# Packed value parts, and edge words turned by DMA instead of TensorE, in a two-layer graph kernel

## The reference, cut to what matters

```python
feats   = einsum('bnf,hfu->bhnu', X, W)                      # 8 heads x 64
dense   = leaky_relu(e_self[:, None] + e_neigh[None, :], 0.2)
att     = softmax(dense + NEG_BIG * (1 - A), axis=-1)        # over neighbours
x       = layernorm(x + relu(att @ feats + b))
deg     = sum(adj, axis=-1)
agg     = (adj @ x) / maximum(deg, 1e-6)
x       = layernorm(x + relu(concat([x, agg]) @ W1.T))
```

## Time and profile before

| | us |
|---|---|
| median of three runs | 3538.81 (3531.39 to 3540.57) |
| the profiled execution | 3539.05 |
| its span on the core | 3537.1 |
| PE busy | 3394.3 (96%) |
| DVE busy | 2461.7 (70%) |
| ACT busy | 1872.3 (53%) |
| POOL busy | 285.1 (8%) |
| mean granted TensorE clock | 0.986 |

### The profile page before, as it was taken

How to read it: one execution, slowest core, us unless ns; L and a number is a source line. 1 busy time by engine, 2 the same in 40 slices (tenths; PEclk the granted TensorE clock), 3 DMA queues, 4 the chain that set the end, 5 groups by cost and what they waited for, 6 DMA issues and landing times.

```text
span 3537.1 us, 135243 instructions
## 1 busy us (share of the span) xinstructions
PE 3394.3 (96%) x58432; PEld 2886.4 (82%) x58432; DVE 2461.7 (70%) x4364; ACT 1872.3 (53%) x2441; POOL 285.1 (8%) x252
## 2 busy tenths in 40 slices
PE   5999999999999999999999999999999999999998
PEld 4978879787796877968789697896978879788795
DVE  4857668576685766858678585785857758576685
ACT  3736546364464645636456363563736537365463
POOL 0020200202001020010201002010020200202001
PEclk9999999999999999999999999999999999999999
DMA  4113031130311303122031220312203131130310
GB/s 170 52 31 128 27 115 57 36 114 23 115 58 46 107 21 118 54 64 89 23 124 45 75 84 20 127 39 83 77 25 128 33 108 52 31 128 27 96 34 24
DMA packets 98396, 248.37 MB, mean 70 GB/s; under 512 B 14720, under 2 KB 14720, under 8 KB 97792
## 3 DMA queue, kind: packets, MB, share of 16 engines
q1 hardware_dynamic: 97792, 239.38, 20.6%
HBM read 205.26 MB, written 34.08 MB: 68 GB/s over the span
## 4 chain that ended last, share of the span: by engine, by line
PE 82%; DVE 9%; issue 5%; DMA 2%; ACT 2%; SPq 0%; DVEq 0%; ACTq 0%; POOL 0%; POOLq 0%
PE six L859 69%; PE pair L859 9%; DVE xs L738 2%; DVE stats L743 2%; PE six L996 2%; DVE feat L630 1%; DMA out_dram<-mask 1%; PE pair L888 1%; PE six L888 1%; DVE rs L751 0%; PE pair L897 0%; ACT x_parts L472 0%; DVE trl L619 0%; PE six L897 0%; DVE nb L753 0%
## 5 line engine op out<-in xcount | busy, mean ns | idle before, releaser
L859 PE MATMUL six<-rest,mask 128*128 128x65 bf16 x16384 | 1554.6, 194 | 3.1 <-issue 2.6
L859 PE MATMUL six<-x_parts,mask 128*128 128x65 bf16 x16384 | 1554.1, 193 | 2.2 <-issue 0.8
L859 PE MATMUL six<-third,mask 128*128 128x65 bf16 x16384 | 1554.1, 193 | 0.2
L859 PEld LDWEIGHTS six<-x_parts,mask 128*128 128x128 fp8e4 x16384 | 1538.2, 97 | 9.7 <-issue 8.0
L859 PEld LDWEIGHTS six<-rest,mask 128*128 128x128 fp8e4 x16384 | 1534.3, 97 | 6.8 <-issue 4.6
L859 PEld LDWEIGHTS six<-third,mask 128*128 128x128 fp8e4 x16384 | 1537.7, 97 | 0.0
L450 ACT ACTIVATE step<-s_bc,n_step 128x1024 uint16<-128x1024 f32 x1024 | 1092.1, 1138 | 369.7 <-DVE mask L688 369.0
L688 DVE TENSOR_TENSOR mask<-adj_t,step 128x1024 uint16<-128x1024 uint16 x1024 | 651.3, 685 | 24.7 <-ACT step L450 24.7
L859 PE MATMUL six<-adj_t,x_parts 128*128 128x512 fp8e4 x1536 | 387.3, 379 | 8.8 <-ACT x_parts L472 6.4
L393 POOL TENSOR_TENSOR s_bc<-feat,rden 128x512 f32<-128x512 f32 x112 | 124.1, 1113 | 3009.6 <-DVE s_bc L731 2980.8
L859 PEld LDWEIGHTS six<-adj_t,x_parts 128*128 128x128 f16 x1536 | 146.1, 98 | 186.4 <-issue 24.9
(11 more groups left out here) (117 smaller groups left out, 4952.0 us busy)
## 6 DMA issues: line engine op xcount, KB each, us to landing
adj_nat<-in_adj_dram SPq DMA_DIRECT2D x128, 512.0 KB, 4.5
s_bc<-self_scores SPq DMA_DIRECT2D x128, 512.0 KB, 3.8
xs<-in_x_dram SPq DMA_DIRECT2D x128, 256.0 KB, 4.1
out_dram<-mask SPq DMA_DIRECT2D x128, 256.0 KB, 3.9
adj_nat<-in_x_dram SPq DMA_DIRECT2D x64, 256.0 KB, 5.2
step<-in_x_dram SPq DMA_DIRECT2D x64, 256.0 KB, 3.7
xs<-in_L_gnn_W_dram SPq DMA_DIRECT2D x1, 2048.0 KB, 11.7
feat<-in_L_gnn_W_dram SPq DMA_DIRECT2D x4, 256.0 KB, 3.6
```

The lines of the kernel that those rows point to most:

```text
L859: return pe.matmul(o, l, r, start=start, stop=stop, skip_group_check=True)
```

## The change

It has three parts.

1. *Packed values.* There is now one f32 pair (`val32`: whole and rest) for all heads, and two sets of packed bf16 parts, with rows of 66 instead of 65 (`packed`). DVE writes the third part into them; ACT copies the upper halves of whole and rest into them: `pack_first_head` (two copies of 520 elements for each half of head 0: one half before step 0, one after step 3) and `pack_head` (one copy of 2080 elements: head 1 after step 10, head h after step 8h). DVE waits for ACT's copies before it overwrites `val32`, PE before it starts a head. A one-element Sigmoid ahead of the first copy loads ACT's table early.
2. *Edge words.* ACT's row-sum copy now multiplies by 0x00C0 and writes 16-bit words into three slots of `adj_word`; SP turns each block with one transposing DMA of 128x1024 words from `adj_word` to `adj_t`. `turn_adj` on PE and `adj_rows` on DVE are gone. The copies for the next batch stand at t = 0, 1, 2, 4, 4, 5, 6 and 7 of stage (3) instead of t = 4 to 7 and the end, with four load slots instead of three.
3. *The loop's end.* `scores(b + 1, 1)` and `features(b + 1, 4)` stand at the end of PE's loop body instead of its top; the scores are made in two pieces, of 384 and 128 columns, and in a bank of their own. DVE's `feature_rows(b, 5)` stands behind the first half of the values of head 0.

```diff
+    WORDS_AT = {0: (0,), 1: (1,), 2: (2,), 4: (3, 4), 5: (5,), 6: (6,)}
@@ sync
+            def turn_adj(b, t):
+                sp.wait_ge(deg_row.sem, deg_row.at(b, t + 1))
+                stand(sp)
+                sp.dma_start_transpose(adj_t[:, :, col(t)],
+                                       adj_word[:, t % WORD_SLOTS, :]).then_inc(adj_turned[t % WORD_SLOTS].sem, 16)
...
                 for t in range(T):
-                    for late in {4: (3, 4), 5: (5, 6), 6: (7,)}.get(t, ()):
-                        load_late_adj(b + 1, late)
+                    if t == 1:
+                        sp.wait_ge(agg_ps.sem, agg_ps.at(b, 2 * KC))
+                    for turned in {1: (0, 1), 2: (2,), 5: (3, 4), 6: (5,), 7: (6,)}.get(t, ()):
+                        turn_adj(b + 1, turned)
+                    for late in {0: (4,), 1: (5,), 2: (6,), 5: (7,)}.get(t, ()):
+                        load_adj(b + 1, late)
...
                 store_y(b, T - 2)
+                turn_adj(b + 1, T - 1)
                 store_y(b, T - 1)
@@ scalar
-            def degrees(b, t):
...
-                act.activation(row_copy[:], adj_nat[:, t % ADJ_SLOTS], ACT.Copy,
+            def adj_words(b, t):
...
+                if t >= WORD_SLOTS:
+                    turned = adj_turned[t % WORD_SLOTS]
+                    act.wait_ge(turned.sem, turned.at(b, 16 * (t // WORD_SLOTS)))
+                act.activation(adj_word[:, t % WORD_SLOTS], adj_rows_at(t), ACT.Copy, scale=float(EDGE),
                                accum_out=deg_sum[:, t:t + 1]).then_inc(deg_row.sem, 1)
...
+                def pack_head(h):
+                    act.wait_ge(val_rest.sem, val_rest.at(b, h + 2))
+                    copy(packed[h % 2][:, 0:2].rearrange("p s k t u -> p (s k t) u")[:, :, 0:U1],
+                         upper_halves.rearrange("p s k t u -> p (s k t) u")).then_inc(val_packed.sem, 1)
...
+                pack_first_head(FIRST)
                 for g in range(H * T):
                     make_step(g)
+                    if g == 3:
+                        pack_first_head(SECOND)
+                    if g == 10:
+                        pack_head(1)
+                    if g >= 2 * T and g % T == 0:
+                        pack_head(g // T)
...
                     if more and t == T - 1:
+                        adj_words(b + 1, 7)
                         act.wait_ge(o2_ps.sem, o2_ps.at(b, T))
                         x_high(b + 1, T - 1)
@@ vector
+                if h >= 1:
+                    dve.wait_ge(val_packed.sem, val_packed.at(b, h + 3))
+                    dve.wait_ge(val_p2.sem, val_p2.at(b, h + 1))
...
-                feature_rows(b, 5)
...
                 value_parts(b, 0, FIRST)
-                dve.wait_ge(at_sb.sem, at_sb.at(b, T))
+                feature_rows(b, 5)
+                all_turned(dve, b)
@@ tensor
-            def turn_adj(b, t):
...
+            def second_half(b):
+                scores(b, 1, slice(0, HALF - 1))
+                scores(b, 1, slice(HALF - 1, HALF))
+                features(b, 4)
...
-                pe.wait_ge(sc_f32.sem, sc_f32.at(b, 1))
-                scores(b, 1)
-                features(b, 4)
                 pe.wait_ge(sc_f32.sem, sc_f32.at(b, 2))
...
                     pe.wait_ge(val_p2.sem, val_p2.at(b, h + 2 if h else 1))
+                    pe.wait_ge(val_packed.sem, val_packed.at(b, h + 4 if h else 2))
...
                 if more:
-                    turn_adj(b + 1, 6)
-                    turn_adj(b + 1, 7)
+                    second_half(b + 1)
                     pe.wait_ge(o2_sb.sem, o2_sb.at(b, T))
                     pe.wait_ge(o_sum.sem, o_sum.at(b, T))
```

163 lines of the change are left out of this document (76 added, 87 removed).

## The result

The changed kernel took 3571.8 us (median of 5 runs, 3557.2 to 3575.2), the kernel before 3533.8 us beside it. The ratio is 1.009, 95% interval 1.0075 to 1.0106. The forecast was 3457 us, a gain; the kernel became slower. The profiled execution took 3574.9 us, span 3572.2 us, 35.1 us more than the span of before.

What follows compares the result with a forecast made beforehand. PE, busy 96% of the span, was taken as the bound. From 3539 us, 69 (transposes, loop's end), 43 (packed reads) and 3 (start) came off and 33 (head 0) went on: 3457 us, range 3385 to 3575.

Steps and rivals of the forecast that it cites:

- Packed reads: Key tile matmuls in heads 1 to 7: 1.0 ns less each, 43 us in 16 batches, bounds 0 and 82.
- Rival A: Key tile matmuls: packing gives PE nothing, so the time is 3500 us; chance 0.17.
- So heads 2 to 7 stay with PE: Heads 2 to 7: PE's 11.8 us a head stays the bound, with ACT's waits hidden and DVE at 10.1.
- I had warned of ACT: Heads: ACT becomes the bound if its copies take twice 2.1 us, about +200 us, 3650; chance 0.04.
- Head 0: From K, the first key tile: PE stands 2.1 us a batch before mask 7, costing 33 us in 16.
- The transposes, the loop's end and the start: Layer 1, loop's end and start: 69 us saved in 15 rounds, plus 3 us at the start.
- Ahead of E: Layer-1 stage up to its end, E: PE loses transposes and the wait for DVE's multiply, 3.5 us saved a round.
- From E to K: End of layer 1 (E) to first key tile (K): 22.8 us against 23.9, worth 1.1 us a round.
- late by some 0.5 us: Behind the loop's branch: DVE is late for the maximum of the scores by 0.5 us, between 0 and 1.5.
- The DMA transpose: Edge words: each transposing DMA lands in 3.9 us; the five ahead of mask 0 need 20 and cost nothing.
- rival C: Five transposes ahead of mask 0: slow transposing DMAs make the kernel slower, 3592 us at 9 us each; chance 0.15.
- The start: Start of the kernel: a DMA chain replaces eight PE transposes, 3 us gained, between 13 gained and 20 lost.

Runs made afterwards that it cites:

- e1: The kernel before, with PE reading the always packed third value part in place of all three: 0.9959 of the kernel before.
- e1b: The kernel before, with PE reading the packed third part for all three and its rows 66 elements apart: 0.9937 of the kernel before.
- e9: The changed kernel without its packing copies and the waits for them, PE reading the third part three times: 0.9924 of the kernel before.
- e10: The changed kernel with head 0's second packing later, block 5's store earlier, and score loads of heads 2 to 7 in four DMAs: 1.0005 of the kernel before.
- e12: e8 with the four 256 KB loads into `step` moved from head 7 to behind the heads: 0.9808 of the kernel before.
- e2: The changed kernel with ACT's copies for head 0's second half after step 7 instead of step 3: 0.9939 of the kernel before.
- e8: The changed kernel with head 0's second packing later, block 5's store earlier, and a 32-byte tile restoring 64-byte alignment: 0.9822 of the kernel before.
- e3: The changed kernel with SP issuing block 5's store ahead of its last wait for a residual: 0.9996 of the kernel before.
- e6: The changed kernel with its 128 transposing DMAs replaced by plain DMAs of the same bytes: 1.0049 of the kernel before.

## Why the prediction was wrong, step by step

The forecast took 82 us off, the profile has 35 us more. Of the 117 between, the heads behind head 0 make 53 (step 2), the loop's end, layer 1 and the start 51 (steps 4 and 6), head 0 with its lower clock 27 (step 3); the faster matmuls give 15 back (step 1).

1. **Packed reads: right, and larger.** 1.0 ns forecast, 1.18 measured, of it 0.9 for packing (e1) and 0.26 for the even pitch (e1b), which the forecast didn't have. Rival A is out. The base price was read wrong: in 10.00 / 326 the 326 counts every matmul that overlaps the stretch, and only 320 start in it, 31.3 ns each and not 30.7. So a steady head took 12.0 us, not 11.8, and the upper bound of this term, 82 us, should have been about 108. That 1.0 ns came near was partly luck: it was half of a difference read too small, and a part of what was measured is the pitch. The Trainium skill's rule (SBUF — State Buffer, "Door 1: The DMA port swizzle"), by which packing gives nothing, does not hold for this read: 31.33 against 30.43 ns.
2. **"So heads 2 to 7 stay with PE": failed, and it is the largest miss by a little.** The step counted engines' busy time and put PE's own supply of instructions at nothing. Its stands inside tiles were 11.3 us before, too small to show in the views that I read; a faster PE reaches each block's end sooner, and they were 25 to 30 us with packed reads in the old kernel (e1, e1b), 23 in e9, 47.6 in the changed one. Blocks that start late behind DMA traffic are what PE waits for, and the loads decide which (e10, e12). How much of the 47.6 the changed order of instructions and loads adds, and how much the chip, stays open. At tile edges the heads behind head 0 added another 17 us. I had warned of ACT, but e9, without any packing copy, keeps 14 of them: it is DVE, in head 3. I compared its 10.1 us of work with 11.8, left out the two splits of x that it makes in each of heads 2 and 3 and its waits for ACT, and took PE's old pace, not the 11.4 that my own first term gave it.
3. **Head 0: 33 us forecast, 45 us of stands and 14 us of lower clock.** The chain was right to 0.2 us: mask 7 at K + 12.8 for the forecast's K + 12.6, PE 2.05 us late for 2.1. Left out was tile 4: mask 4 came at K + 6.4, and PE wanted it at K + 5.8. Left out as well was the clock, which fell behind these stands in 9 batches. With the second packing four steps later 7.5 us of the stands are left, and the clock stays up behind them (e2).
4. **The transposes, the loop's end and the start: 72 us forecast, 21 in the profile, 5 between e9 and e1b.** Ahead of E it was 2.65 us a round for 3.5; slower matmuls on the shifted tiles took 0.7 of the missing 0.85 (e8). From E to K it was 0.9 us worse where 1.1 better was forecast. The step that failed is DVE "late by some 0.5 us", with 1.5 as its bound: it was late by 1.87 in the round shown and 2.0 in the mean, since its turn of the loop (3.56 us) starts only behind a wait for a store (3.02 us), which stood in SP's queue behind a wait for the residual. With that store first, E to K is 22.0 us (e3), below the forecast's 22.8. The clock fell as assumed (0.50 from 1399.9 to 1406). The narrow score matmuls cost another 0.7 us that I had priced by their columns. ACT's turn, 4.01 us, with a table load behind it was not counted at all; the chain was checked from the small transposes on, not from the branch.
5. **The DMA transpose: right.** 3.4 us to landing for 3.9 assumed, so rival C is out. With plain copies in their place the time is 14 us lower (e6), a part of which may be the chip's. Of the Trainium skill's two answers the one that forecast slow transposes (VectorE: DVE Perf Modes, "The three transpose paths"; I estimated 10.5 us from it) is not what these rows show; "X-Bar Transpose (TRN2)" in Advanced Engine Details and Errata, by which they are as fast as others, agrees with them.
6. **The start: forecast 3 us better, 3.2 us worse.** The first key tile is at 91.4 us (88.2 before). It is between 89.9 and 92.5 us in all profiles with transposing DMAs, and at 88.8 with plain copies (e6). So the DMA chain costs as much there as the transposes on PE did, or a little more; the term was a guess between 13 gained and 20 lost.

## What to carry to other kernels

When an engine that bounds a kernel is to become faster, compare its new pace, not its old one, with every engine that feeds it, and look in the trace for its instruction packets and what DMA traffic lies ahead of them: what has a few tenths of slack in 12 us loses them by the change's own success. Before work is put into an in-order queue, list what stands behind it and when each is wanted; here one copy four places later, and one store one place earlier, turned a loss of 0.9% into a gain of 1.5%. At this loop's branch ACT took 4.0 us to turn and DVE 3.6, each for itself, so look there for whatever is last to arrive, and what its last wait is for.

## What the runs showed of the hardware

- A bf16 moving operand of 65 columns read from every second word costs 31.33 ns a matmul, packed 30.43, with rows an even number of elements apart 30.17.
- The 512-column f32 matmuls on `w1l`, with a moving tile that starts 32 bytes off a multiple of 64, took 234.2 to 234.7 ns from start to start, and 227.0 to 229.2 on it (before, e8). Others followed in part (`w1h` on `x1t_h` 231.5 off it and 230.8 on it) or not at all (`w0`), so the rule is not complete.
- Score matmuls of 384 columns came every 176 ns, those of 128 every 116 ns, where a quarter of the 227 ns of 512 would be 57: the last are not set by their columns.
- PE's instructions came in DMA packets of 16,384 bytes, one for each 124 or 125 matmuls with their weight loads, and 1.2 to 1.6 us passed from the end of a late packet to PE's next matmul. Stands of up to 2.1 us came from packets that began late, with the DMA engines busy for 65% of the 2.5 us before them (11% ahead of the others). Four 128 KB loads in place of one of 512 KB raised these stands from 39.0 to 94.8 us.
- A transposing DMA of 128 x 1024 two-byte words landed in 3.4 us (median of 128; 3.1 to 6.0) and took 1.24 us on the queue that issues it (median; up to 2.7).
- The branch of this loop took 4.01 us on ACT and 3.56 on DVE in the round shown.
